# An encoder of four attention blocks on one core: the decoder opens with one token tile, and half of the last cross sums is taken inside the phase

## What is computed

```
def step(t, p):
    tn = _ln(t, norm_g, norm_b)
    t = _mha(tn, tn, skv, sq, sow, sob, tgt_mask) + t
    tn = _ln(t, norm_g, norm_b)
    t = _mha(src, tn, ckv, cq, cow, cob, src_mask) + t
    tn = _ln(t, pg, pb)
    t = t + (jax.nn.relu(tn @ w1 + b1) @ w2 + b2)
```

## Time and profile before

| what | us |
|---|---|
| three runs | 1040.49, 1040.86, 1041.80 |
| median | 1040.86 |
| the profiled execution | 1041.94 |
| its span | 1039.90 |
| PE busy in it | 1018.5 (98%) |
| DVE, ACT, POOL busy | 715.5, 801.0, 407.7 |

### The profile page before, as it was taken

One profiled execution on the slowest core, in us unless ns is written; L12 is line 12 of the kernel. 1 busy time (PEld: TensorE's weight loads), 2 busy tenths in 40 slices (PEclk: granted clock), 3 DMA queues, 4 the chain that ended last, 5 costly groups with the idle time before them and its releaser, 6 DMA issues.

```text
span 1039.9 us, 22180 instructions
## 1 busy us (share of the span) xinstructions
PE 1018.5 (98%) x5980; PEld 683.0 (66%) x5980; DVE 715.5 (69%) x4485; ACT 801.0 (77%) x3527; POOL 407.7 (39%) x419
## 2 busy tenths in 40 slices
PE   8899999999999999999999999999999999999996
PEld 6655567766568766558875557876646876655885
DVE  4666787567778566778665578766678856677955
ACT  4787998667988676899676799867798868689852
POOL 4233543233544233454333354323354424354432
PEclk9999999999999999999999999999999999999999
DMA  8412000004000003200002200000400000000000
GB/s 232 113 62 70 2 22 1 2 1 123 29 21 2 1 2 82 70 1 21 2 1 74 76 2 21 1 2 4 133 16 22 1 2 1 21 1 1 2 1 24
DMA packets 31957, 32.89 MB, mean 32 GB/s; under 512 B 4008, under 2 KB 27730, under 8 KB 31058
## 3 DMA queue, kind: packets, MB, share of 16 engines
q1 hardware_dynamic: 29522, 29.19, 9.8%
q10 hardware_dynamic: 2304, 2.20, 0.6%
HBM read 30.86 MB, written 0.52 MB: 30 GB/s over the span
## 4 chain that ended last, share of the span: by engine, by line
PE 95%; DVE 2%; issue 1%; ACT 1%; DVEq 0%; POOL 0%; POOLq 0%
PE S L1104 26%; PE T L1116 13%; PE sum L1160 12%; PE W L916 9%; PE sum L1130 8%; PE W L940 4%; PE W L971 4%; PE W L858 3%; PE W L895 3%; PE W L878 2%; PE W L873 2%; PE W L935 2%; PE W L837 2%; PE W L849 2%; PE W L827 1%
## 5 line engine op out<-in xcount | busy, mean ns | idle before, releaser
L1405 ACT ACTIVATE Pb<-Pb,mn 128x128 f32<-128x128 f32 (+1 forms) x1536 | 560.6, 370 | 51.6 <-DVE mn L1640 51.4
L722 POOL TENSOR_TENSOR Pb<-Pb,rsum 128x512 f32<-128x512 f32 (+2 forms) x336 | 325.0, 969 | 552.2 <-DVE rsum L1648 552.2
L1405 ACT ACTIVATION_READ_ACCUMULATOR Pb<-Pb,mn 128x1 f32 x1536 | 293.1, 191 | 0.0
L1640 DVE CUSTOM_DVE_ANT_0 Pb<-S,late_bias 128x128 f32<-128x128 f32 x768 | 175.6, 285 | 125.9 <-PE S L1104 125.0
L1116 PEld LDWEIGHTS T<-ident,Pb 128*128 128x128 f32 (+2 forms) x1296 | 163.3, 147 | 127.4 <-issue 105.1
L1104 PE MATMUL S<-GV,XT 128*128 128x512 f32 x384 | 200.3, 608 | 2.6 <-issue 1.8
L1116 PE MATMUL T<-ident,Pb 128*128 128x128 f32 (+2 forms) x1296 | 196.9, 273 | 0.2
L1658 DVE COPY PT<-T 128x512 f32<-128x512 f32 (+1 forms) x240 | 156.5, 652 | 45.5 <-PE T L1116 44.4
L1640 DVE CUSTOM_DVE_ANT_0 Pb<-S,cross_bias 128x77 f32<-128x77 f32 x768 | 132.3, 232 | 55.7 <-PE S L1104 53.5
L1160 PEld LDWEIGHTS sum<-Vc,PT 128*128 128x128 f32 (+2 forms) x1056 | 131.4, 190 | 21.3 <-issue 18.7
L1160 PE MATMUL sum<-Vc,PT 128*128 128x128 f32 (+2 forms) x1056 | 139.1, 276 | 0.0
(11 more groups left out here) (213 smaller groups left out, 1063.7 us busy)
## 6 DMA issues: line engine op xcount, KB each, us to landing
sakv<-in_L_xattn_sa_kv SPq DMA_DIRECT2D x6, 1024.0 KB, 4.9
caq<-in_L_xattn_ca_q SPq DMA_DIRECT2D x6, 512.0 KB, 8.4
saq<-in_L_xattn_sa_q SPq DMA_DIRECT2D x6, 512.0 KB, 7.0
cakv<-in_L_xattn_ca_kv SPq DMA_DIRECT2D x12, 256.0 KB, 8.0
saow<-in_L_xattn_sa_ow SPq DMA_DIRECT2D x6, 512.0 KB, 4.0
w<-in_L_xattn_ff_w SPq DMA_DIRECT2D x12, 256.0 KB, 3.1
caow<-in_L_xattn_ca_ow SPq DMA_DIRECT2D x30, 96.0 KB, 2.6
GV<-in_mask_BxSxS_ik ACTq DMA_DIRECT2D x1, 1536.0 KB, 9.3
```

The source lines that it names most:

```text
L722: nc.gpsimd.tensor_tensor(rows, rows, r, ALU.mult).then_inc(sem(f"{unit.name}_weights"), 1)
L1405: last = nc.scalar.activation(Pb[:, s, t * w:(t + 1) * w], Pb[:, s, t * w:(t + 1) * w], ACT.Exp, bias=mn[:, s, t:t + 1], scale=-1.0, accum ...
L1640: last = nc.vector.tensor_tensor_reduce(out=Pb[:, s, cols], in0=S_ps[n % 2][:, cols], in1=row_bias, scale=1.0, scalar=3.4e38, op0=ALU.add, ...
```

## The change

Three things are changed.

**The opening.** The last token tile of batch 0 (LATE, the only one with keys) is led through L1 by itself: its scores, exponentials, turn, values, residual and layer norm come ahead of the three others (OTHERS). Its transpose is a new event ("late", 0, 0) of the prologue's ring, so that "k" of the first layer, "G" and "v" stand before the "xn" of the other three tiles. The rest of batch 1's L1 (exponentials, turn, values, residual, layer norm) moves into the decoder's first ticks as `opening`. Two squares of the mask move ahead of ACT's first token copy. POOL adds the biases in three pieces. The loads of saq, the norms and sakv are issued ahead of small_rows and caq.

**The tables.** Most offsets are changed by one to three ticks.

**The end.** After six of the last phase's twelve chunks the sums of batch 1's first two tiles are complete. DVE adds them, norms them, and PE turns them ("half") within the phase. L3's values of batch 0 move into the phase too. The ending has one filler group less (`keep(12)`), other banks, and interleaves the halves.

```
-CV0_AT = (10, 12, 15, 16, 24, 27)
-CV_AT = (4, 6, 7, 20, 26, 29)
-SELF1_AT = (23, 24, 26, 30)
-SELF0_AT = (18, 18, 26, 29)
-WEIGHTS0_AT = (5, 3, 7, 12, 16, 18)
-WEIGHTS_AT = (20, 23, 30, 32, 33, 33, 35, 35, 37, 37, 40, 40, 43, 42, 45, 45)
-AFTER_S0 = (3, 4, 5, 5, 6, 7)
+FIRST_AT = (0, 1, 0, 4, 5, 6, 2)
+OPEN_AT = (0, 1, 3)
+XN1_AT = (6, 7, 9, 11)
+CV0_AT = (14, 17, 19, 20, 25, 31)
+CV_AT = (4, 6, 7, 20, 26, 28)
+SELF1_AT = (23, 24, 26, 32)
+SELF0_AT = (17, 17, 26, 28)
+WEIGHTS0_AT = (3, 2, 5, 10, 14, 16)
+WEIGHTS_AT = (18, 21, 28, 30, 31, 31, 33, 33, 35, 35, 38, 38, 41, 40, 43, 43)
+AFTER_S0 = (3, 4, 8, 8, 9, 10)
...
-AFTER_X0 = (2, 2, 3, 4, 5, 7)
+AFTER_X0 = (2, 2, 3, 4, 5, 6)
...
-LAST_AT = (1, 3, 5, 9)
-FEED0 = ((8, 8, 9, 9), 10, (13, 14, 15, 17))
-FEED1 = ((9, 9, 9, 9), 12, (18, 18, 20, 21))
+HALF_AT = (13, 16, 18, 20, 24)
+LAST_AT = (1, 3, 6, 8)
+FEED0 = ((7, 7, 7, 7), 8, (11, 12, 13, 15))
+FEED1 = ((10, 9, 9, 9), 14, (18, 18, 20, 21))
...
+        self.jobs[1 + kept].append(("k", 0, 0, 0))
+        self.jobs[1 + turned] += [("G", 0, 0, 0, 0), ("G", 0, 0, 0, 1)]
+        self.jobs[1 + rest].append(("xn", 0, 0, 0))
...
+        for what, dt in zip(("exps", "turn", "values"), OPEN_AT, strict=True):
+            self.opening[1 + dt].append(what)
...
+                for what, dt in zip(("added", "spread", "normed"), HALF_AT):
+                    self.half[x1 + dt].append(what)
+                self.jobs[x1 + HALF_AT[3]].append(("half", j, 1))
+                self.jobs[x1 + HALF_AT[4]].append(("p3", self.layers, 0))
...
+            keep(2)
+            second_turn(0, LATE, sum_ps, 1)
             second_tokens(1)
-            keep(1, sum_ps)
+            keep(1)
             pe.wait_ge(sem("L1_vo_sb"), 1)
-            second_values(0)
-            second_scores(1)
-            pre(*PRE_TQ, ("small", 0))
-            keep(2, sum_ps)
+            second_values(0, LATE, S_ps[0], 1)
+            second_turn(0, OTHERS, T_ps[0], 2)
             pe.wait_ge(sem("bad_rows"), 1)
             pe.wait_ge(sem("unmasked"), SQUARES)
...
-            keep(4, sum_ps)
-            second_turn(1)
+            pre(*PRE_TQ)
+            second_values(0, OTHERS, T_ps[0], 2)
             keep(2, sum_ps)
-            second_values(1)
+            second_scores(1)
+            pre(("small", 0))
+            keep(3, sum_ps)
+            pre(PRE_X, *PRE_CQ)
...
+                    if at_end and group.first and qt == TB // 2:
+                        pe.wait_ge(sem("tail_sums_read"), 1)
...
-                pe.wait_ge(sem("L3_vo"), 1)
-                token_values("L3", 0, W_ps[0]).then_inc(sem("tail_pred"), 1)
-                keep(12)
...
+                made(FAST.ring, [("half", L - 1, 1)], 0)
+                hidden(0)
+                pe.wait_ge(sem("tail_sums_read"), 2)
+                output(0)
+                keep(2, T_ps[1])
```

More of the change, by code:

```diff
@@ L186, in __init__ @@
         self.norm = [[] for _ in range(self.ticks)]
+        self.half = [[] for _ in range(self.ticks)]
+        self.opening = [[] for _ in range(self.ticks)]
         self.evict_o = [[] for _ in range(self.ticks)]
@@ L726, in decoder @@
                                  l * len(unit.norms) + unit.norms.index(event) + 1)
+                    for what in unit.half[t]:
+                        if what == "spread":
+                            root("tail", tiles2(0), 1)
                     for event, step in unit.norm[t - 1] if t > 0 else []:
@@ L741, in ending @@
             def ending():
[L743 to L749, removed]
+                add_b2(0)
+                root("tail", tiles2(1), 2)
+                add_b2(1)
                 root("tail", slice(0, TB), 3)
@@ L932, in work @@
                     else:
-                        pe.wait_ge(sem("start_norm"), B + b + 1)
-                    for t in range(TB):
-                        last = nc.tensor.transpose(w[:, t * P:(t + 1) * P], XN[:, b * TB + t, :], ident[:])
+                        for t in range(2):
+                            nc.tensor.matmul(w[:, t * P:(t + 1) * P], ident[:], ident[:], start=True, stop=True)
+                        pe.wait_ge(sem("start_norm"), B + 2)
+                        tokens = range(TB - 1)
+                    for t in tokens:
+                        last = nc.tensor.transpose(w[:, t * P:(t + 1) * P], XN[:, b * TB + t, :], ident[:])
+                elif what == "late":
+                    made(ring, [], l, fills)
+                    pe.wait_ge(sem("start_norm"), B + 1)
+                    last = nc.tensor.transpose(w[:, 0:P], XN[:, TB - 1, :], ident[:])
+                elif what == "half":
+                    made(ring, [], l, fills)
+                    pe.wait_ge(sem("tail_norm"), 1)
+                    for t in range(TB // 2):
+                        last = nc.tensor.transpose(w[:, t * P:(t + 1) * P], XN[:, TB + t, :], ident[:])
                 elif what == "h":
@@ L1179, in decoder @@
                         work(ring, event, l, unit)
+                    for what in unit.opening[t]:
+                        opening(what)
                 for k in range(ring.banks):
@@ L1232, in _ @@
             with pe.Else():
+                opening("turn")
+                opening("values")
                 with pe.Fori(0, L) as l:
@@ L1424, in decoder @@
                         work(ring, event, l, unit)
+                    for what in unit.opening[t - 1] if t > 0 else []:
+                        opening(what)
                     for what, b in unit.late[t]:
@@ L1465, in _ @@
             with act.Else():
+                opening("exps")
+                opening("turn")
                 with act.Fori(0, L) as l:
```

312 lines of the change are left out of this document (185 added, 127 removed).

## The result

| what | before | after |
|---|---|---|
| median of 20 executions, us | 1042.03 | 1043.62 |
| lowest, highest | 1040.49, 1045.00 | 1042.25, 1047.80 |
| the profiled execution, its span | 1041.94, 1039.90 | 1042.25, 1040.36 |
| TensorE clock of the profiled span | 0.998 | 0.997 |

The ratio of after to before is 1.0022, 95% interval 1.0015 to 1.0030: 2.3 us slower. (By the medians it is 1.6 us.) The median of after is above the forecast's range (1034.9 to 1041.2), and it moved the other way. The profiled execution of after is the quickest of its 20, so the two profiles differ by 0.3 only (0.5 by their spans).

What follows compares the result with a forecast made beforehand. TensorE, busy 98% of the span, was taken as the bound. Opening -2.7, layers -0.5 and end +0.2 gave -3.0 us: profiled 1038.9, median 1037.9; stated range 1034.9 to 1041.2, the forecast's own 1035.5 to 1039.9.

Steps and rivals of the forecast that it cites:

- The opening: Start of the program up to the fourth turn: first scores 3.5 us sooner, less returned work and waits, -2.7 us.
- rival C: Opening: full ACT and added DVE work give the lead back; opening only -0.5, median 1040.1; chance 0.21.
- the change takes two stretches out from ahead of 'k': PE's opening: 2.54 us (batch 1's turn, values) and 1.58 us (four transposes, a copy wait) vanish before "k".
- the flag's product: Opening: it must wait for the mask's last square, now behind ACT's exponentials; priced at 0.6 us, between 0 and 0.96.
- PE's waits there stay as they are: Opening's first chunks up to the fourth turn: PE's waits unchanged despite 3.2 us more DVE work, being set by ACT.
- The layers: Five layers: -1.0 us from sums placed between scores, +0.5 from later vTb copies; together -0.5 us.
- Rival D: Layers: vTb copies ahead of XN make PE wait at feed forward's transposes, 1.1 us per layer, median 1043.4; chance 0.10.
- The end: Last phase and ending: -3.2 + 1.1 + 1.6 + 0.7 = +0.2 us.
- the gain of 3.2: After the last sum: first half no longer waits, so the path to the scores is 10.7 us instead of 13.86.
- copy behind "s3", weights behind the root: Last phase: turned weights' copy behind "s3" and statistics, POOL's root ahead of a weight step; +1.6 us.
- XN beside POOL: Last phase: XN loses part, not all, of a POOL step's time, +0.4 us, with the copy behind it +0.7.
- The sum: Whole kernel: -2.7 - 0.5 + 0.2 = -3.0 us, median 1037.9, 0.3% faster.

Runs made afterwards that it cites:

- the tables by halves: Kernel before with only CV_AT, SELF1_AT, SELF0_AT, WEIGHTS_AT changed, then only AFTER_S0, AFTER_X0, FEED0, FEED1; one execution each: 1047.97 and 1045.85 us beside 1041.83.
- the tables alone: Kernel before with only the change's layer offset tables, its opening and end untouched: 1043.12 us, ratio 1.0011.
- the version with before's tables: The change with before's offset tables, batch 1's root moved back, POOL's additions held until XN, four fillers ahead of L0's second values: 1039.83 us, ratio 0.9983 to before.

## Why the prediction was wrong

**The opening** was forecast at -2.7, with G at 33.7 and the first scores at 37.0. They came at 34.47 and 37.91 (the pieces on PE between "k" and the scores were sized rightly, within 0.2 each). The fourth turn came at 55.26, between the forecast's 54 and rival C's 56. Three steps failed.

- The step "the change takes two stretches out from ahead of 'k'" counted what leaves PE and asked only ACT's square for a new wait. It did not follow the late tile's chain back through DVE to POOL, though the change moves the root of batch 1's norm on POOL behind a wait for a load. That made 1.74 us of idle PE, 2.81 in another execution. Its price in the plan was nothing. The wait I did price, 0.6 for the flag's product, was 0.32.
- "PE's waits there stay as they are" for the first chunks: at 52.70 and 55.26 it waited 0.31 for XN and 0.64 for POOL's weights. Before, it had 0.49 near 48 us in that stretch, so this is about 0.5 more. The lead at the first scores, 2.6, less values of 0.9 and these 0.5, is about the 1.1 seen at 90 us. A part of rival C's mechanism, but POOL and DVE were the ones waited for, not ACT.
- No term at all stood for the clock. The prediction's windows of before show 1.00, and took PE's idle time in the opening as costing its own length. In the change, 10 of 20 executions have a clock of 0.993 or 0.994, and eight of these are 1.5 to 5.2 us above 1042.6, the middle of the six quickest. This is most of why the median lost 1.6 where the profile lost 0.3; filling the stretches took about 1 us off.

**The layers** were forecast at -0.5 and took +0.8. The gain where a layer begins came. PE's loss there was 1.0 by the earlier trace rows; after, it is one wait:

```profile
196.70 0.66 PE L1172 MATMUL T<-ident,Pb 128*128 128x128 f32 x4
197.99 1.96 PE L1160 MATMUL S<-GV,XT 128*128 128x512 f32 x4 [0.63 <-ACT GV L1354]
```

From 196.70 to 197.99 are 1.29 with four transposes of 0.11 in them, so 0.85 is lost, 0.15 to 0.2 less, as forecast. The 0.3 to 0.4 a layer that went the other way stands at the place shown with the tables by halves: batch 0's norm, put later by `AFTER_S0` and beside POOL's weights, and the copy of o_pair behind it. The step that failed is that the sum had no term for this norm at all. It took moved work off PE's path as free and looked at the norm ahead of the feed forward only. That PE changes more often between kinds of product, the theory of the runs by halves, is not so: from G to G it changes tile or shape 255 times before and 256 times in the change.

**Rival D** did not come. Its slack was forecast at 0.26; XN was done at 497.62 + 0.85 = 498.47 and PE came to it at 499.42, so 0.95 was left:

```profile
499.42 0.60 PE L974 MATMUL W<-ident,XN 128*128 128x128 f32 x4
```

```profile
497.62 0.85 DVE L1586 TENSOR_SCALAR XN<-X,mv,rstd 128x128 f32<-128x128 f32 x3
```

**The end** was forecast at +0.2 and took +0.5 in the whole, while alone it gained 0.3. From the last sum, which ends at 1015.81 by the row, to the span's end are 24.55 us, where 23.9 was forecast: the gain of 3.2 was 2.5. PE waits 0.66, 0.35 and 0.47 for ACT's hidden rows and copies, which the sum had at 3.0 together with all other hops. That sum has a slip too: 3.4, 3.5, 0.4 and twice 0.4 make 8.1 and not 7.7, and with 8.1 the gain would have been 2.8. Within the phase the last sum ends 2.94 later than before (1012.87): 1.1 for the values and two transposes, as forecast, 1.06 of waits at the named places (copy behind "s3", weights behind the root) where 1.6 and 0.7 more for XN were forecast, and 0.8 in small pieces that no term named. So the near hit of the end's sum is partly luck: the gain was put too high, and the delays too. The term that the prediction left to the row, XN beside POOL, went by the Trainium skill's rule (SBUF — State Buffer, "Who interferes with whom": the shared port pair is an exclusive lock for the whole instruction). XN started at 1009.67 beside POOL's weights (1009.60 to 1010.56) and took 0.97; the next started at 1010.56. It had waited out POOL's operation, not a part of it. The row before was in accord with that too: 1.02 for two tiles are the 0.68 to the end of POOL's addition (1016.72 + 0.73) and one XN of 0.34. I had read the difference of 0.41 as a share and not asked where POOL's operation ends. Not every operation of POOL does this: before, two XN at 1016.04 took their 0.61 beside a root of 0.70 that began at 1015.99, and the tables alone show the same. By the page's rule the prediction had put the end at +0.7; the measured +0.5 lies between that and +0.2, and since the other terms were off as well, it speaks for neither.

**The sum** missed on the side, not only in size. The rival that ends slower was looked for in the layers (D), where a slack could be computed, and not in the opening, where an engine queue had been reordered behind a load.

## What to carry to other kernels

Follow every wait of the chain that a change puts first back through all its engines, and read the queue of each: an operation that nobody moved on purpose (here a root on POOL) can be behind a load now. Where a kernel carries fillers to keep TensorE's clock, price new idle time there not at its length but at what the lower clock costs after it, and look at the spread of the executions, since a single profile may show the good one. Tables of offsets that were tuned together are to be judged together. A loss of a few tenths a layer is found by lining up the starts of the same products in both programs, where a list of idle times over 0.3 us shows nothing.

## What the runs showed of the hardware

- With TensorE idle for 2.81 us in the opening, the granted clock fell to 0.50 about 2 us after the idle time's end, for about ten us. With 1.45 us of idle time ahead of 15.05 us it did so from about 15.8 us on, and with 0.93 and 0.85 us at that place it was 0.66 in the window 15:20. The length of the idle time does not settle it: the change kept a clock of 1.00 behind 1.74 us in its profiled execution, and the tables alone behind 1.34 us ahead of L0's first values.
- With products that nobody reads in both stretches, no execution of 11 had a clock under 0.997. In the version with before's tables, whose second stretch was shortened by other means, four such products in the first left none of 11 under 0.996. The kernel before has 6 of 91 at 0.994 or less.
- VectorE's `XN` (a tensor_scalar) and GpSimd's additions and weight steps (tensor_tensor) do not share time: in each of the four places looked at, XN ended or its successor began at the end of GpSimd's operation (22.30, 446.28, 1010.56, and 1017.45 + 0.34 before). Three XN took 0.85 alone, 1.66 and 2.10 beside GpSimd. Beside a root of 0.70 (a tensor_tensor on 128x2) two XN lost nothing.
